# The last three dense experts go through the tokens group by group, and each group's layer norm runs in the same stage

## What is computed

```python
def _layernorm(x, axis=-1, eps=1e-05):
    m = jnp.mean(x, axis=axis, keepdims=True)
    v = jnp.var(x, axis=axis, keepdims=True)
    return (x - m) / jnp.sqrt(v + eps)
...
    shared = jax.nn.relu(xt @ sW1 + sb1) @ sW2 + sb2
    ...
    h = jax.nn.relu(jnp.einsum('nd,edh->neh', xt, eW1) + eb1)
    ye = jnp.einsum('neh,ehd->ned', h, eW2) + eb2
    routed = jnp.einsum('ned,ne->nd', ye, cw)
...
    x = x + jnp.tanh(g_ffn[2]) * _L2_ffn_ref(_layernorm(x, axis=-1), ...)
    x = x + jnp.tanh(g_xattn[3]) * _L3_xattn_ref(_layernorm(x, axis=-1), ...)
```

## Time and profile before

| | us |
|---|---|
| time, median of 3 runs | 1626.92 (1626.75 to 1629.39) |
| the profiled execution, its own time | 1622.71 |
| its span in the trace | 1620.9 |
| mean granted TensorE clock | 0.895 of full speed |
| busy, TensorE / VectorE / ScalarE / GpSimd | 1379.8 / 1062.6 / 778.8 / 649.0 |

### The profile page before, as it was taken

The page is one execution under the profiler, slowest core; times in us unless marked ns, Lnnn a source line. Parts: engine busy times, 40 slices in busy tenths (PEclk is TensorE's granted clock), DMA queues, the critical chain, the costliest instruction groups (busy, mean ns, idle before and its releaser), DMA issues. The chain is left out here.

```text
span 1620.9 us, 29634 instructions
## 1 busy us (share of the span) xinstructions
PE 1379.8 (85%) x10158; PEld 739.9 (46%) x10166; DVE 1062.6 (66%) x3273; ACT 778.8 (48%) x1105; POOL 649.0 (40%) x505
## 2 busy tenths in 40 slices
PE   5999965749999999998339999997999489999981
PEld 3444453615666666666313333333677223333431
DVE  4887744166676666764688777763556787777725
ACT  3777721336665665654113555554433125555550
POOL 4666613514676666777632112200600432332000
PEclk7999976958999999999557999998899769999995
DMA  4566623535342233400054334401200133223001
GB/s 140 193 238 233 241 88 118 157 123 214 143 151 90 101 143 145 155 1 1 17 118 78 75 73 110 86 2 45 48 1 1 25 49 54 38 42 59 13 2 29
DMA packets 87990, 147.57 MB, mean 91 GB/s; under 512 B 15875, under 2 KB 61086, under 8 KB 84261
## 3 DMA queue, kind: packets, MB, share of 16 engines
q1 hardware_dynamic: 84510, 116.94, 25.9%
q10 hardware_dynamic: 1824, 25.17, 4.0%
q0 software_dynamic: 1520, 3.68, 0.9%
HBM read 93.66 MB, written 45.11 MB: 86 GB/s over the span
## 5 line engine op out<-in xcount | busy, mean ns | idle before, releaser
L1834 DVE CUSTOM_DVE_ANT_0 a_junk<-a_psM,a_madd 128x512 bf16<-128x512 f32 x512 | 332.2, 683 | 92.1 <-issue 89.4
L1780 ACT ACTIVATE a_probs<-a_psE 128x1024 f32<-128x1024 f32 x256 | 262.0, 1023 | 214.8 <-PE a_psE L1669 213.9
L2235 DVE TENSOR_REDUCE a_mx<-a_psM 128x1 f32<-128x512 f32 x236 | 148.1, 668 | 124.2 <-PE a_psM L2060 124.2
L1669 PE MATMUL a_psE<-a_maddT,res_identb 64*128 64x512 bf16 x1024 | 221.8, 388 | 2.1
L1646 PE MATMUL a_psM<-narrow_k_op,narrow_q_op 57*128 57x512 bf16 (+1 forms) x512 | 153.0, 415 | 42.1 <-DMA narrow_q_op<-a_y_parts 20.3
L2197 ACT ACTIVATE a_probs<-a_psE 128x1024 f32<-128x1024 f32 x128 | 130.8, 1024 | 85.3 <-PE a_psE L2082 82.0
L190 POOL TENSOR_SCALAR res_xn<-res_X,res_mv,n_rstd 128x128 f32<-128x128 f32 x32 | 26.8, 847 | 352.9 <-DVE n_rstd L176 352.9
L1680 PE MATMUL a_psO<-a_probs,narrow_values 128*32 128x256 f32 x2048 | 164.0, 394 | 2.5 <-ACT a_probs L1780 1.1
L2030 POOL TENSOR_TENSOR a_half_sum<-a_probs 128x1024 f32<-128x1024 f32 x64 | 150.8, 2356 | 32.9 <-ACT a_probs L2197 32.7
L2078 PE MATMUL a_psE<-a_qT,a_kT 64*128 64x256 f32 x1024 | 133.4, 380 | 0.0
L2094 PE MATMUL a_psO<-a_probs,a_values 128*64 128x256 f32 x1024 | 124.6, 385 | 0.8 <-ACT a_o_raw L2181 0.8
(11 more groups left out here) (334 smaller groups left out, 2528.4 us busy)
## 6 DMA issues: line engine op xcount, KB each, us to landing
wide_k<-a_k_stage SPq DMA_DIRECT2D x32, 512.0 KB, 3.2
wide_v<-a_v_stage SPq DMA_DIRECT2D x32, 512.0 KB, 4.3
a_k_part<-wide_k SPq DMA_DIRECT2D x64, 256.0 KB, 3.4
a_kT<-wide_k ACTq DMA_DIRECT2D x6, 2048.0 KB, 8.2
a_values<-wide_v ACTq DMA_DIRECT2D x6, 2048.0 KB, 8.6
keys<-a_parts SPq DMA_DIRECT2D x96, 64.0 KB, 2.0
narrow_q_op<-a_y_parts SPq DMA_DIRECT2D x192, 32.0 KB
narrow_k_op<-keys SPq DMA_DIRECT2D x30, 192.0 KB
```

The lines of the kernel that those rows point to most:

```text
L1669: return pe.matmul(psE[s % 2][:, j, :, :], res.identb[group, :], maddT[r][group, s % 2 * 2:s % 2 * 2 + 2, :], start=False, stop=last, skip ...
L1780: act.activation(probs[:, head:head + 2, k:k + 2, :], psE[s % 2][:], ACT.Exp).then_inc(exped, 1)
L1834: dve.tensor_tensor_reduce(junk[j][:], psM[j][:], madd[r][:, t, :], 1.0, -3.0e38, ALU.add, ALU.max, mx[r][:, max_place(h, t):max_place(h, ...
L2235: dve.tensor_reduce(mx[r][:, at:at + 1], max_bank(2 * p + t, j, first), AX.X, ALU.max).then_inc(max_read, 1)
```

## The change

The steps are ordered by a list. The first 13 experts go as before. For the last three (`LAST`) the groups are outside and the experts inside: steps 52, 53, 54 are experts 13, 14, 15 on group 0, steps 55 to 57 the same on group 1, and so on. The norm stage n6 is gone; a helper `NormTail` does its work in the expert stage. For each group VectorE forms variance plus epsilon and the negated mean (`moments`, two instructions on 128x4) behind the statistics, and four instructions on 128x4 (`vector`) one group later, behind the additions of the next group's first step. ScalarE takes the root of a group (`root`), then normalises two tiles of the group before in two passes each (`scalar`: subtract the mean, then scale), then copies out the transposes of the one before that (`copy`). GpSimd normalises the other two tiles (`gpsimd`). TensorE transposes a group (`tensor`) into psH[0] or psH[1], behind the last `give` of the next group. VectorE waits for its own additions before each step of experts 14 and 15, which now add to the same tiles as the step just before.

```diff
+class NormTail:
...
+    def moments(self, dve, c):
+        four = slice(4 * c, 4 * c + 4)
+        dve.tensor_scalar(self.var[:, four], self.res.mv[:, four, 1], LN_EPS, None, ALU.add).then_inc(self.ready, 1)
+        dve.tensor_scalar(self.away[:, four], self.res.mv[:, four, 0], -1.0, None, ALU.mult).then_inc(self.ready, 1)
...
+    def root(self, act, c):
+        four = slice(4 * c, 4 * c + 4)
+        act.wait_ge(self.ready, 2 * c + 2)
+        act.activation(self.std[:, four], self.var[:, four], ACT.Sqrt).then_inc(self.rooted, 1)
+
+    def scalar(self, act, c):
+        res = self.res
+        act.wait_ge(self.newton, 4 * c + 4)
+        for t in (4 * c, 4 * c + 1):
+            act.activation(res.xn[:, t, :], res.X[:, t, :], ACT.Identity, bias=self.away[:, t:t + 1]).then_inc(self.shifted, 1)
+        for k in range(2):
+            t = 4 * c + k
+            act.wait_ge(self.shifted, 2 * c + k + 1)
+            act.activation(res.xn[:, t, :], res.xn[:, t, :], ACT.Copy, scale=self.rstd[:, t:t + 1]).then_inc(self.by_act, 1)
+
+    def tensor(self, pe, c):
+        if c >= 2:
+            pe.wait_ge(self.copied, c - 1)
+        pe.wait_ge(self.by_act, 2 * c + 2)
+        pe.wait_ge(self.by_pool, 2 * c + 2)
+        for k in range(4):
+            last = pe.transpose(self.psT[c % 2][:, k * P:(k + 1) * P], self.res.xn[:, 4 * c + k, :], self.res.ident[:])
+        last.then_inc(self.turned, 1)
...
-    LEAD, H_RING, B2_TURN = 3, 3, 6
+    LEAD, H_RING, B2_TURN, LAST = 3, 3, 6, 3
+    whole = E - LAST
+    order = [(e, c) for e in range(whole) for c in range(NCHUNK)] + [(e, c) for c in range(NCHUNK) for e in range(whole, E)]
...
+                    for m, (e, c) in enumerate(order):
+                        give(m, e, c)
...
+                        if e == E - 1 and c >= 1:
+                            norm.tensor(pe, c - 1)
+                    norm.tensor(pe, NCHUNK - 1)
...
+                    for c in range(NCHUNK):
+                        norm.root(act, c)
+                        if c >= 1:
+                            norm.scalar(act, c - 1)
+                        if c >= 2:
+                            norm.copy(act, c - 2)
+                    norm.scalar(act, NCHUNK - 1)
+                    norm.copy(act, NCHUNK - 2)
+                    norm.copy(act, NCHUNK - 1)
...
+                    for m, (e, c) in enumerate(order):
+                        if e > whole:
+                            dve.wait_ge(added, m)
+                        dve.wait_ge(made, m + 1)
...
+                            tile_stats(dve, res, 4 * c, 4, 4 * c, stats_done, aggr_done)
+                            dve.wait_ge(aggr_done, 4 * c + 4)
+                            norm.moments(dve, c)
+                        if e == whole and c >= 1:
+                            norm.vector(dve, c - 1)
+                    norm.vector(dve, NCHUNK - 1)
...
+                    for c in range(NCHUNK):
+                        norm.gpsimd(pool, c)
...
-                norm_phase(nc, io, res, "n6")
```

More of the change, by code:

```diff
@@ L1123, with __init__, vector, gpsimd @@
 L2_EXPERTS, L2_LOADS = 16, 4
+class NormTail:
+    def __init__(self, ph, res, psT):
+        self.res, self.psT = res, psT
+        self.var, self.r0, self.rr, self.half, self.rstd, self.away = (
+            ph.sb(f"tail_{n}", [P, NTILE]) for n in ("var", "r0", "rr", "half", "rstd", "away"))
+        self.std, self.ready, self.rooted = ph.sb("tail_std", [P, NTILE]), ph.sem("tail_ready"), ph.sem("tail_rooted")
+        self.newton, self.shifted, self.by_act, self.by_pool = (ph.sem(f"tail_{n}") for n in ("newton", "shifted", "by_act", "by_pool"))
+        self.turned, self.copied = ph.sem("tail_turned"), ph.sem("tail_copied")
+    def moments(self, dve, c):
+        four = slice(4 * c, 4 * c + 4)
+        dve.tensor_scalar(self.var[:, four], self.res.mv[:, four, 1], LN_EPS, None, ALU.add).then_inc(self.ready, 1)
+        dve.tensor_scalar(self.away[:, four], self.res.mv[:, four, 0], -1.0, None, ALU.mult).then_inc(self.ready, 1)
+    def vector(self, dve, c):
+        newton, four = self.newton, slice(4 * c, 4 * c + 4)
+        var, r0, rr, half, rstd = (a[:, four] for a in (self.var, self.r0, self.rr, self.half, self.rstd))
+        dve.wait_ge(self.rooted, c + 1)
+        dve.reciprocal(r0, self.std[:, four]).then_inc(newton, 1)
+        dve.wait_ge(newton, 4 * c + 1)
+        dve.tensor_tensor(rr, r0, r0, ALU.mult).then_inc(newton, 1)
+        dve.wait_ge(newton, 4 * c + 2)
+        dve.scalar_tensor_tensor(half, rr, -0.5, var, ALU.mult, ALU.mult).then_inc(newton, 1)
+        dve.wait_ge(newton, 4 * c + 3)
+        dve.scalar_tensor_tensor(rstd, half, 1.5, r0, ALU.add, ALU.mult).then_inc(newton, 1)
+    def gpsimd(self, pool, c):
+        res = self.res
+        pool.wait_ge(self.newton, 4 * c + 4)
+        for t in (4 * c + 2, 4 * c + 3):
+            pool.tensor_scalar(res.xn[:, t, :], res.X[:, t, :], res.mv[:, t, 0:1], self.rstd[:, t:t + 1],
+                               ALU.subtract, ALU.mult).then_inc(self.by_pool, 1)
+    def root(self, act, c):
[3 more added lines that the diff above has]
+    def scalar(self, act, c):
+        res = self.res
+        act.wait_ge(self.newton, 4 * c + 4)
[13 more added lines that the diff above has]
+        last.then_inc(self.turned, 1)
+    def copy(self, act, c):
+        act.wait_ge(self.turned, c + 1)
+        act.copy(self.res.xnT[:, c * CHUNK:(c + 1) * CHUNK], self.psT[c % 2][:]).then_inc(self.copied, 1)
@@ L1169, in layer2_experts @@
             psB = ph.ps("psB", [P, 4, D])
+            norm = NormTail(ph, res, psH[0:2])
             hidden, acted, made, added = (ph.sem(n) for n in ("hidden", "acted", "made", "added"))
@@ L1182, in hide, with give @@
                         pe.matmul(psH[n % H_RING][:], w1[:, e, :], res.xnT[:, c * CHUNK:(c + 1) * CHUNK], start=True, stop=True).then_inc(hidden, 1)
-                    def give(e, c):
-                        m = e * NCHUNK + c
-                        pe.wait_ge(acted, m + 1)
+                    def give(m, e, c):
+                        pe.wait_ge(acted, e * NCHUNK + c + 1)
                         if m >= 2:
@@ L1212, in _ @@
                             hide(e, c)
[L1213 to L1221, removed]
+                    for m, (e, c) in enumerate(order):
+                        give(m, e, c)
+                        if e + LEAD < E:
+                            hide(e + LEAD, c)
+                        if e == B2_TURN:
+                            turn_combine(c)
+                        if e == B2_TURN + 1:
+                            output_bias(c)
+                        if e == E - 1 and c >= 1:
+                            norm.tensor(pe, c - 1)
+                    norm.tensor(pe, NCHUNK - 1)
                 @block.scalar
@@ L1245, in _ @@
                     router.vector(dve)
[L1246 to L1262, removed]
```

13 lines of the change are left out of this document (12 added, 1 removed).

## The result

| | before | changed |
|---|---|---|
| time, median of 6 runs, us | 1627.84 (1626.61 to 1629.39) | 1635.6 (1634.03 to 1637.49) |
| the profiled execution, its own time | 1622.71 | 1634.28 |
| its span | 1620.9 | 1632.5 |
| mean granted TensorE clock | 0.895 | 0.904 |
| from step 52's first addition to the last copy of `res.xnT` | 28.0 | 35.45 |

The changed kernel is slower: the ratio is 1.005, with an interval of 1.0039 to 1.0062, or +7.8 us between the medians. The profiled executions lie 11.6 us apart, and 3.5 of these lie ahead of step 52, which starts at 1254.70 and started at 1251.23, in stages that the change does not touch. The last row of the table leaves that out. It gives +7.45 us. Behind it the next stage starts 0.38 us after the last copy (0.52 before). From the last copy to the end of the span it is 342.35 us, where it was 341.68.

The account below looks back on a forecast made before the run. VectorE and TensorE wait on each other, then a one-engine-at-a-time chain; 8.8 us removed, but tail 5.4, stalls 4.6, `vector`s 2.7 and `moments` 1.2, less some filled idle time, give +9.2: 1636.1 us. Range: 1632.0 less 0.5 to 1636.8 plus 1.7.

Parts of the forecast that it names:

- What bounds it, and group 0: End of expert stage and norm: 8.8 us behind the last aggregates removable; group 0's `moments` end at 1256.4, table load hidden.
- Group 1: Steps 55 to 57 with group 0's `vector`, statistics and `moments`: 5.8 us, ending at 1262.2.
- The stall: Before steps 58 and 61, TensorE's transposes wait for ScalarE behind the next group's root, holding VectorE: two stalls, 4.6 us.
- The clock: TensorE's clock after standing still: low for the transposes and step 58, high for the end of step 60.
- Groups 2 and 3: Cycles from step 58's additions on: 10.4 us each, ending at 1272.6 and 1283.0.
- The tail: Root, ScalarE's passes for groups 2 and 3, transposes and copies after group 3's `moments`: 5.4 us, ending at 1288.4.
- The own waits: VectorE waiting for its own additions in the last experts' steps: 0.12 us a step.
- rival 1: No stall before step 58: groups follow every 5.8 us, time stays the same at 1626.9; chance 0.08.
- rival 2: Stall is there but TensorE stays at the high clock: slower by 5.1 to 6.2 us, 1632 to 1633; chance 0.24.
- rival 3: Attention stage behind runs at a higher clock, up to 11.4 us saved: -5.2 us, about 1621.7; chance 0.04.
- rival 4: Change doesn't do what it says; norm of group 3 and half of group 2 stays behind the last expert, 5.4 us.
- signs named for a wrong forecast: VectorE's idle pieces under 1 us, or the stage behind differing from its 300 us by more than 1 us.

Follow-up runs that it names:

- e4: Changed kernel plus 28 extra identity transposes on TensorE ahead of each wait for a normalised group; 1626.07 us against 1618.72 for the kernel before, ratio 1.004.
- e1: Changed kernel with ScalarE normalising group c-1's two tiles before the root of group c; 1618.97 us against 1618.72 for the kernel before, ratio 0.9998.
- e2: Changed kernel with each group's transposes on TensorE one group later, ScalarE's order kept; 1618.0 us against 1618.72 for the kernel before, ratio 0.9993.
- e5: Changed kernel with LAST = 1: steps in the old order, only the norm moved into the expert stage; 1627.54 us against 1620.51 before, ratio 1.0046.
- e7: Changed kernel with ScalarE's tiles before the next root, later transposes, last group's four tiles on VectorE; 1617.89 us against 1620.51 before, ratio 0.9988.

## Why the prediction was right

The forecast was 1636.1 us and +9.2 us; measured were 1635.6 and +7.8 between the medians, 7.45 in the trace. The two absolute numbers agree better than the sum deserves: the kernel before ran 0.9 us longer in the runs of the comparison than in those that the sum started from, and the sum was 1.4 us too large. By its own steps:

- **What bounds it, and group 0.** The `moments` of group 0 end 1259.93 - 1254.70 = 5.23 us behind step 52's start; the forecast's 1256.4 meant 5.2. The table load is hidden, right behind the last relu, as said, and there is only one.
- **Group 1.** Forecast 5.8, measured 5.5. The term that was too large is `vector`, at 0.9: it took 1261.56 - 1260.88 = 0.68. The four instructions start 0.20 apart on 128x4, where rows 1 had 0.28 and 0.21 on 128x16. I had seen the smaller shape and left the price.
- **The stall.** Forecast 4.6 (its terms add up to 4.46), measured 4.32, twice, and by the chain that was named: `moments` of group 1, root, two tiles, transposes, `give`. Its pieces: 0.04 to the root, 0.11 to the first pass (the root itself, 0.20 long, overlaps it; forecast 0.25), 1.26 for the passes (1.3), 0.05 of handover (0.16), 0.91 and 1.95 for transposes, `give` and handover at the low clock (0.9 and 1.85). In this trace ScalarE's first pass on a tile of group 0 starts 10.9 us after step 52's additions; the forecast said 11. That TensorE would idle some 5 us before each set of transposes held for three of the four; before the last it idled 0.63.
- **The clock.** Low for the transposes and step 58, high for step 60, as forecast. e4 gives its share: 1.27 us a stall, against the 1.2 that the forecast has between its 1265.5 and 1266.7. The page "TensorE: Matmul & The Clock Gate" of the Trainium skill, section "HAM oscillation", lets each burst behind a pause pay. The trace agrees for the opening of each burst, and step 60 at 1.00 shows that here not the whole of it does.
- **Groups 2 and 3.** Forecast 10.4 each, measured 9.93: the shorter `vector` and the shorter stall.
- **The tail.** Forecast 5.4, measured 1290.15 - 1285.29 = 4.86; ScalarE's passes for two groups run without a gap, and overlap at each change of form.
- **The own waits.** Forecast 0.12 each; two steps with one between them take 2.29 where rows 1 have 2.16, so 0.13. The page "VectorE: DVE Perf Modes" of the Trainium skill, section "The DRAIN you can't avoid", has a semaphore behind each instruction cost nothing extra, and adds that an instruction that is not held starts earlier. The trace doesn't agree with the first: the wait costs 0.13 here. It fits the second: the two independent `moments` of 0.17 start 0.08 apart, and the chained instructions of `vector` 0.20 apart.

The terms that were too large add up to the miss: 0.3 + 2 x 0.47 + 0.54 = 1.8 us, which is 9.2 less 7.45. Some of this is rounding: the tail's terms add up to 5.3 and not 5.4, and all terms unrounded give +9.0 and not +9.2.

The rivals: that the stall isn't there (rival 1) has its decisive row at 1265.59, behind group 1's aggregates at 1265.17, so it is false. Its second half was right: in e1 and e2, where the stall is gone or nearly so, the time is that of before. A stall at the high clock (rival 2) is false in the changed kernel and is what e4's trace shows, with 4.5 us in the stretch where the rival had 5.1 to 6.2. The faster stage behind (rival 3) is false by its clock of 0.51 in 1307 to 1335. That group 3's norm stays behind the last expert (rival 4) is the tail of 4.86.

One of the signs named for a wrong forecast did appear: the stage behind took 1.1 us more, and the limit was 1 us. With 302.3 to 304.4 us in the traces of the experiments, that limit was narrower than the spread of this stage, so the sign decides nothing.

What stays open: the 3.5 us by which the two profiled executions differ ahead of step 52. In the nine traces of this case step 52 starts between 1246.44 and 1254.70, though what stands ahead of it is the same in all, so 3.5 us lie within the spread. The medians differ by 7.8, close to the stretch's 7.45. What makes this spread isn't known; no run was made for it.

## What to carry to other kernels

When work of group c - 1 is slipped into in-order queues between the steps of group c, write down for each queue what stands in front of it: here one root too early on ScalarE and one set of transposes too early on TensorE cost 8.8 us together, and moving either removed the stalls, the first but for 0.95 us. Where each group has only one step left (e5), the place on TensorE was enough. Engines that were idle don't make such work free. What a removed stage really costs is its chain behind the last input; if that chain remains for the last group, only the rest can be won, and the small instructions per group are paid from it.

## What was not expected of the hardware

**The clock fell in a pause of 1.3 us, too.** e1 in stretches:

```profile
1254.00:1256.00 2.00, 1.13 (x8) 0.97 (x8) 1.86 (x10) 1.17 (x4) 1.02 (x2) 1.00 0.00 0
1256.00:1258.00 2.00, 1.29 (x6) 1.32 (x7) 1.93 (x9) 0.11 (x1) 0.57 (x1) 0.55 0.03 8
1258.00:1260.00 2.00, 2.00 (x13) 2.00 (x12) 1.02 (x8) 0.20 (x1) 0.00 (x0) 0.60 0.00 0
```

TensorE was idle for 1.31 us, and for 1.49 us shortly before, and the clock was 0.55 and 0.60 in the next two stretches. Later in the same kernel pauses of 1.21 us left it at 1.00, and in e2 a pause of 1.49 did. In e7 a pause of 1.21 us did not: the stretch from 1266 to 1268 has 0.56, and the transposes in it took 1.09 us. So in these traces the length of one pause doesn't tell which way it goes.

**It did not fall at one distance behind the last product either.** In the changed kernel TensorE ends a burst at 1262.23, at 1272.16 and at 1282.09, each time ahead of 4.67 to 4.71 us of idle time. The stretch right behind the first end has 0.75, shown above; later ones behind the other two:

```profile
1274.00:1276.00 2.00, 0.00 (x0) 0.00 (x0) 1.30 (x10) 0.60 (x3) 0.00 (x0) 1.00 0.00 0
1276.00:1278.00 2.00, 1.17 (x6) 1.18 (x7) 0.00 (x0) 1.24 (x4) 0.00 (x0) 0.67 0.04 8
...
1284.00:1286.00 2.00, 0.00 (x0) 0.00 (x0) 1.59 (x13) 0.67 (x3) 0.00 (x0) 1.00 0.00 0
1286.00:1288.00 2.00, 1.01 (x4) 0.64 (x4) 0.30 (x2) 2.00 (x8) 1.57 (x2) 0.73 0.00 0
```

In two cases the clock stayed high for over 3.8 us of the pause, and in the first it fell within 1.8 us. Two things set these apart in the rows: the idle time ahead of the last product, 1.50 us in the first case, 0.30 and 0.15 in the others, and when the clock had last risen, long before the first case, but only some 2 us before the end of the burst in the others. No run was made to test either. The clock was low when the transposes of groups 0 and 1 started, so the two stalls are equal; those of group 2 started at 1286.80, just ahead of the fall, and took 1.01 us instead of 1.11.
